# A scan without a barrier ahead of it: f32 spreads, paired sums, and the first scan tiles started inside the norm stage

## The chip, the cores and the metric

The kernel runs on one NeuronCore of one Trainium2 chip. The core has five engines with a queue each: PE (TensorE, matmuls into the eight PSUM banks), DVE (VectorE), ACT (ScalarE), POOL (GpSimd) and SP (which issues DMAs here). They run side by side and wait for each other through semaphores only. The metric is device time in microseconds from the first to the last instruction of one execution. Lower is better.

## The reference, cut to what matters

```python
def ssm(seq, A, W_B, b_B, W_C, b_C, W_Delta, b_Delta, bias_Delta):
    Bm = seq @ W_B.T + b_B
    Cm = seq @ W_C.T + b_C
    Delta = jax.nn.softplus(seq @ W_Delta.T + b_Delta + bias_Delta)
    A_bar = jnp.exp(A[None, None] * Delta[..., None])
    B_bar = 1.0 / A * (A_bar - 1.0) * Bm[..., None, :]
    # state = state * A_bar + x[..., None] * B_bar;  y = sum over the 16 states of state * Cm
...
x = sequence                                   # 1 x 4096 x 256, f32
x = x + ssm(layernorm(x), ...)                 # 256 channels of 16 states each, 4096 steps
x = x + ffn(layernorm(x), ...)                 # sqrt((x @ cos)^2 + (x @ sin)^2)
x = x + attention(layernorm(x), ...)           # 16 heads of 16
x = x + ffn(layernorm(x), ...)
```

The change lies in the first line alone, the layer norm with its projections and the scan. All else is computed by the same instructions before and after.

## The kernel before, in words

**The norm stage** (`norm_and_project`, a block of its own with a barrier at its end) goes over the 4096 rows in 8 chunks of 512. DVE takes mean and deviation and normalises. PE turns the chunk (`turn`, L393, eight 128x128 transposes) and multiplies it by the weights of B, C and Delta (L408, six f32 products of 512 columns, the trace shows each f32 product as two rows). ACT copies the turned chunk out of PSUM (L330), then adds the biases on the way out of the projections (`outputs`, L344, three a chunk). Three more steps a chunk make the turned chunk into three bf16 parts, `mem.xp`, whose sum is the f32 value: ACT rounds (`high` L334, `middle` L338), POOL subtracts (`what_hi_leaves` L212), DVE subtracts (`low` L247). The softplus of Delta is made by quarters of 1024 steps: `minus_abs` on DVE (L254), Exp and Ln on ACT (L350, L354), `softplus` on DVE (L259). DVE also makes the angles of the FFN weights (`angles`, `in_range`, L278 to L289).

**The scan** (`scan_to_projection`) has 128 tiles, n = 0 to 127. A tile is 8 channels x 16 states on the 128 partitions and 1024 steps on the free axis. Tile n is quarter n // 32, and its channels are the group j = n % 32. 16 tiles make a half, which is one block of 128 output channels. Its steps for tile n are:

- `spread_x` (PE, L717): a 0/1 matrix copies the 8 channels of x onto 128 partitions, in PSUM. Six bf16 products (three parts, two banks). It goes to one pair of banks, `xr`, for nearly all tiles, so that spread m + 1 waits until DVE has read spread m (`w_done`).
- `times_b` (DVE, L969): w = spread x times B.
- decay (ACT, L871): exp(A Delta) into PSUM, and for the tiles that POOL takes, exp(A Delta) - 1 in SBUF (L857, L860).
- u = w (decay - 1): by POOL (L1113), or by DVE (`own_u`, L980) where n % 8 is 0, 3 or 6, and for the last tile.
- scan (DVE, L999), then hc = state times C (POOL, L1122).
- gather (PE, L749): a 128x32 matrix of 1 / A sums the 16 states of each channel into `yb`, two f32 products of 512 columns, four rows. Four tiles in turn add into the same 32 partitions.
- After 16 tiles ACT copies y (L833), PE turns it (`turn_y`, L728), DVE adds it to x (`add_y`, L964).

The order on each queue is the order of the code. DVE does scan n, then `own_u` of n + 1 if it is DVE's, then `times_b` of n + 4. Near the start of a half two `times_b` stand around one `own_u` (after scan 5 of the half). PE does spread n + 5, then gather n. The named functions `scan_before`, `spread_after` and `by_pool` set these distances.

Of the kernel before, what the change touches and what calls it, by code (L numbers as in the profile page):

```python
# [131 lines left out]
def norm_and_project(nc, mem, io):  # L132

    with ExitStack() as ctx:
        def sb(name, shape, dt):
            return ctx.enter_context(nc.sbuf_tensor(name, shape, dt))

        w_bcd = place(mem, 136, [DH, 3, P])
        bias = sb("bias_bcd", [P, 4], F32)
        recip_a = sb("recip_a", [P, NJ], F32)  # L140
        mask = sb("channel_mask", [P, CPT], F32)
        xn = place(mem, 112, [2, TPC, D])
        xnt = place(mem, 120, [2, DH, CH])
        rest = place(mem, 128, [2, DH, CH])
        std = sb("np_std", [P, NT, 1], F32)
        noise = place(mem, 140, [DH, 2, D])
        turns = place(mem, 144, [DH, 2, D])
        ang = mem.w_ffn[:].rearrange("p h (a o) -> p h a o", a=2)
        tp = ctx.enter_context(nc.psum_tensor("np_tp", [P, DH, CH], F32))
        pb = ctx.enter_context(nc.psum_tensor("np_proj", [P, 2, 3, CH], F32))  # L150
        (loaded, consts, pool_step, gather_step, sums_done, stats_done, std_ready, rstd_ready, xn_ready, t_ready, xnt_ready,
         hi_ready, rest_ready, mid_ready, lo_ready, proj_ready, proj_read, neg_ready, exp_ready, ln_ready, bias_ready,
         soft_added, angles_loaded, angle_step, table_step) = make_sems(
            nc, ctx, "np", "loaded consts poolstep gatherstep sums stats std rstd xn t xnt hi rest mid lo proj projread neg "
            "exp ln bias softadded anglesloaded anglestep tablestep")
        x_loaded = make_sems(nc, ctx, "np", " ".join(f"x{i}" for i in range(NC)))

        def tiles(i):
            return slice(i * TPC, (i + 1) * TPC)

        def cols(i):
            return slice(i * CH, (i + 1) * CH)

        def quarter(q):
            return slice(q * SC, (q + 1) * SC)

        with nc.Block() as block:
            @block.sync
            def _(sp):
                xv = io.x.rearrange("a (t p) d -> (a p) t d", p=P)  # L170
                for i in range(NC):
                    sp.dma_start(mem.x[:, tiles(i), :], xv[:, tiles(i), :]).then_inc(x_loaded[i], 16)
                    if i == 0:
                        sp.dma_start(w_bcd, io.w_bcd.rearrange("(h p) j c -> p h j c", p=P)).then_inc(loaded, 16)
                        sp.dma_start(bias[:], io.bias_bcd).then_inc(loaded, 16)
                        sp.dma_start(mem.a_scale[:], io.a_tiles).then_inc(loaded, 16)
                for n, (w, e) in enumerate(((io.theta, io.theta_noise), (io.phi, io.phi_noise))):
                    sp.dma_start(ang[:, :, n, :], w.rearrange("(h p) o -> p h o", p=P)).then_inc(angles_loaded, 16)
                    sp.dma_start(noise[:, :, n, :], e.rearrange("(h p) o -> p h o", p=P)).then_inc(angles_loaded, 16)

            @block.gpsimd
            def _(pool):
                steps = Chain(pool, pool_step)

# [22 lines left out]
                def what_hi_leaves(i):  # L207

                    pool.wait_ge(hi_ready, i + 1)
                    if i >= 2:  # L210
                        pool.wait_ge(lo_ready, i - 1)
# [403 lines left out]
def scan_to_projection(nc, mem, io, ctx):  # L615
# [91 lines left out]
    def tensor(pe):  # L707
# [23 lines left out]
        for n in range(4):  # L731
            spread_x(n)
# [1103 lines left out]
```

## Time and profile before

| What | us |
|---|---|
| median of 3 runs | 3477.23 (3475.85 to 3478.11) |
| profiled execution, its time | 3478.46 |
| its span, first to last instruction | 3476.6 |
| norm stage, until the barrier | 0 to 77.2 |
| first four scans begin at | 83.5, 88.0, 97.9, 102.4 |
| last scan begins at | 593.2 |
| all that follows (FFN, attention, FFN) | about 609 to 3476.6 |

The table is read from left to right as stages that follow each other. The trace gives for each instruction its start, its engine, its duration, and what ended the idle time of its engine before it.

### The profile page before, as it was taken

What the parts mean: (1) busy time and instruction counts of PE and PEld (TensorE: products, weight loads), DVE (VectorE), ACT (ScalarE), POOL (GpSimd) and SP (SyncE); (2) the same over time, 40 slices, a digit from 0 to 9 for tenths busy, and PEclk for the clock granted to TensorE, in tenths of its full rate; (3) what the DMA queues carried; (4) which work ended last, traced back from release to release, by engine and by line L of the source; (5) the groups of instructions that cost most, each with busy time, mean ns of one, the idle gap of its engine ahead of it and who ended that gap; (6) DMA issues with size and microseconds to landing.
All of it is one profiled execution on the core that took longest, in us unless ns stands there. A gap on an engine that the chain in (4) does not pass through costs nothing.

```text
span 3476.6 us, 59741 instructions
## 1 busy us (share of the span) xinstructions
PE 3330.3 (96%) x22826; PEld 1192.6 (34%) x22852; DVE 3260.1 (94%) x4960; ACT 2718.5 (78%) x4991; POOL 830.4 (24%) x707
## 2 busy tenths in 40 slices
PE   6788888989999999999999999999999999999999
PEld 3222222542333333333333333333333333333334
DVE  7899999589999999999999999999999999999943
ACT  6766665756888888888888888888888888888865
POOL 3899998662000000000000000000000000000004
PEclk9999999988999999999999999999999999999999
DMA  2000001052020120202020202112020202020011
GB/s 65 1 10 0 1 1 49 31 149 30 6 33 13 28 30 10 33 6 33 8 33 6 33 6 33 25 16 33 6 33 6 36 6 33 6 33 6 8 55 49
DMA packets 53678, 87.11 MB, mean 25 GB/s; under 512 B 13200, under 2 KB 40464, under 8 KB 49232
## 3 DMA queue, kind: packets, MB, share of 16 engines
q1 hardware_dynamic: 53200, 82.77, 12.6%
q8 instruction: 179, 2.93, 0.4%
q14 instruction: 107, 0.88, 0.1%
q10 hardware_dynamic: 192, 0.52, 0.1%
HBM read 53.37 MB, written 21.23 MB: 21 GB/s over the span
## 4 chain that ended last, share of the span: by engine, by line
PE 81%; DVE 10%; issue 4%; POOL 1%; ACT 1%; DMA 0%; DVEq 0%; SPq 0%; POOLq 0%; ACTq 0%
PE banks L1493 29%; PE banks L1450 16%; PE banks L1445 15%; PE banks L1408 11%; DVE arena L999 5%; PE banks L553 3%; DVE arena L969 3%; PE banks L1406 2%; PE banks L805 1%; DVE arena L1666 1%; DVE arena L980 1%; PE banks L797 1%; PE banks L1515 1%; POOL arena L1122 0%; POOL arena L1113 0%
## 5 line engine op out<-in xcount | busy, mean ns | idle before, releaser
L1649 DVE TENSOR_REDUCE arena<-banks 128x1 f32<-128x512 f32 x4032 | 2503.7, 683 | 19.1 <-PE banks L1408 15.5
L1623 ACT ACTIVATE arena<-banks 128x512 f32<-128x512 f32 x4096 | 2114.9, 602 | 417.0 <-PE banks L1445 409.5
L1445 PE MATMUL banks<-arena 64*128 64x512 bf16 x4032 | 1245.8, 379 | 0.0
L1450 PE MATMUL banks<-arena 35*128 35x512 bf16 x4032 | 1207.2, 378 | 0.6 <-DMA arena<-max_rows 0.4
L1493 PE MATMUL banks<-arena 128*32 128x512 f32 x8192 | 1090.8, 605 | 0.0
L1406 PE MATMUL banks<-arena 64*128 64x512 bf16 x2048 | 789.2, 387 | 22.9 <-DVE arena L1666 20.2
L1408 PE MATMUL banks<-arena 64*128 64x512 bf16 x2048 | 786.9, 386 | 0.6 <-DVE arena L1649 0.6
L1445 PEld LDWEIGHTS banks<-arena 64*128 64x128 bf16 x4032 | 375.8, 93 | 391.7 <-PE banks L1450 5.7
L1408 PEld LDWEIGHTS banks<-arena 64*128 64x128 bf16 x2048 | 188.2, 93 | 796.6 <-DVE arena L1649 792.4
L1450 PEld LDWEIGHTS banks<-arena 35*128 35x128 bf16 x4032 | 358.0, 93 | 157.7 <-ACT arena L1623 8.7
L1373 POOL TENSOR_TENSOR arena<-arena 64x512 f32<-64x512 f32 x64 | 81.2, 1268 | 1191.6 <-DMA arena<-arena 1157.2
L1122 POOL TENSOR_TENSOR arena<-arena 128x1024 f32<-128x1024 f32 x128 | 301.7, 2369 | 30.3 <-DVE arena L999 30.0
L1341 POOL CAST neg_parts<-neg_max 128x8 bf16<-128x8 f32 x64 | 12.2, 191 | 1239.3 <-DVE neg_max L1661 1239.3
L999 DVE TENSOR_TENSOR_SCAN arena<-banks,carry,arena 128x1024 f32<-128x1024 f32 x128 | 299.2, 2338 | 1.0 <-POOL arena L1122 1.0
L749 PE MATMUL banks<-arena 128*32 128x512 f32 x512 | 247.7, 607 | 41.2 <-POOL arena L1122 41.2
L871 ACT ACTIVATE banks<-arena,a_scale 128x1024 f32<-128x1024 f32 x128 | 142.8, 1116 | 142.3 <-DVE arena L999 141.6
L1493 PEld LDWEIGHTS banks<-arena 128*32 128x32 f32 x8192 | 161.2, 108 | 237.9 <-issue 230.8
L717 PE MATMUL banks<-arena 128*128 128x512 bf16 x742 | 189.6, 389 | 51.7 <-DVE arena L969 39.2
L1406 PEld LDWEIGHTS banks<-arena 64*128 64x128 bf16 x2048 | 190.9, 94 | 52.8 <-DVE arena L1666 26.8
L1113 POOL TENSOR_TENSOR arena<-arena 128x1024 f32<-128x1024 f32 x79 | 189.0, 2393 | 15.3 <-DVE arena L969 15.3
L969 DVE TENSOR_TENSOR arena<-banks,arena 128x1024 f32<-128x1024 f32 x128 | 154.0, 1204 | 11.9 <-PE banks L717 11.9
L717 PEld LDWEIGHTS banks<-arena 128*128 128x128 bf16 x768 | 65.9, 99 | 219.0 <-DVE arena L969 121.6
(137 smaller groups left out, 1730.7 us busy)
## 6 DMA issues: line engine op xcount, KB each, us to landing
arena<-qk_parts SPq DMA_DIRECT2D x242, 128.0 KB, 7.1
qk_parts<-arena SPq DMA_DIRECT2D x32, 384.0 KB, 2.6
arena<-arena SPq DMA_DIRECT2D x63, 128.0 KB, 2.3
x_res<-in_x SPq DMA_DIRECT2D x8, 512.0 KB, 7.9
arena<-in_trig SPq DMA_DIRECT2D x2, 2048.0 KB, 9.0
arena<-qk_parts SPq DMA_DIRECT2D x64, 64.0 KB, 10.9
att_t<-arena SPq DMA_DIRECT2D x128, 32.0 KB
arena<-att_t SPq DMA_DIRECT2D x8, 512.0 KB, 5.5
```

What stands on the lines that cost most here:

```text
L717: last = nc.tensor.matmul(x_bank(n)[:, b * CH:(b + 1) * CH], mem.spread[:, j % NJH, :], mem.xp[:, part, j // NJH, c * SC + b * CH:c * SC + ...
L749: last = nc.tensor.matmul(yb[32 * g:32 * g + 32, b * CH:(b + 1) * CH], mem.gather[:, j, :], hc[:, n % 2, b * CH:(b + 1) * CH], start=(r == ...
L969: nc.vector.tensor_tensor(w[:, n % WBUF, :], x_bank(n), mem.b_rep[:, cols(n)], ALU.mult).then_inc(w_done, 1)
L999: nc.vector.tensor_tensor_scan(st[:, n % 2, :], decay[:, n % 2, :], w[:, n % WBUF, :], mem.carry[:, j:j + 1], ALU.mult, ALU.add).then_inc( ...
L1122: nc.gpsimd.tensor_tensor(hc[:, n % 2, :], st[:, n % 2, :], mem.c_rep[:, cols(n)], ALU.mult).then_inc(hc_done, 1)
L1406: return nc.tensor.matmul(out, q_twin[LANE:P, par, q], k_twin[LANE:P, par, c // 2, :], start=True, stop=True)
L1408: return nc.tensor.matmul(out, q_rows[0:LANE, par, q], k_rows[0:LANE, par, c * CH:(c + 1) * CH], start=True, stop=True)
L1445: return nc.tensor.matmul(sc[:, (4 * t + j) % SB, :], k, q, start=(j == 1), stop=(j != 1))
L1450: return nc.tensor.matmul(sc[:, (4 * t + j) % SB, :], k, q, start=(j != 1), stop=(j == 1))
L1493: last = nc.tensor.matmul(acc[32 * j:32 * j + VW, :], v_ones[:, h % 2, 2 * kp + j // 2, :], prob[:, t % PBUF, j * CH:(j + 1) * CH], start= ...
L1623: nc.scalar.activation(prob[:, t % PBUF, j * CH:(j + 1) * CH], sc[:, n % SB, :], ACT.Exp, scale=SCALE).then_inc(exp_done, 1)
L1649: nc.vector.tensor_reduce(part_max[:, b % 2, u // NC, u % NC:u % NC + 1], mx[:, unit_bank(b, u), :], AXX, ALU.max).then_inc(dve_read, 1)
```

## The change

It does these things:

1. The barrier between norm stage and scan is gone. The norm stage is now the first part of the one block that holds all else, and its semaphores (`mem.norm`) order the seam. It uses the PSUM banks of the scan: projections in banks 0 to 5, turned chunks in 6 and 7.
2. The turned chunk stays f32 in `mem.x_t`, and ACT copies it there straight from PSUM. `high`, `middle`, `what_hi_leaves` and `low` are gone. A spread is two f32 products (four rows) where it was six bf16 products.
3. At the seam PE does spread 0 (into banks 6 and 7) ahead of the projection of chunk 7. ACT does decay 0 ahead of the `outputs` of chunk 7. `minus_abs` of the last quarter moves behind scan 1 on DVE.
4. u of tile 1 is DVE's, so u of the first two tiles is.
5. The 16 tiles of a half run in another order of channel groups (`channels`): tile n and n + 1 now sum into different 32 partitions of `yb`. The gathers of two tiles stand together, bank by bank, behind the odd one (`sum_pair`), and hc has four buffers for two.

```diff
@@ norm_and_project
-            nc.scalar.activation(xnt[:, i % 2], tp[:], ACT.Copy).then_inc(xnt_ready, 1)
-        def high(i):
...
+        act.wait_ge(t_ready, i + 1)
+        nc.scalar.activation(mem.x_t[:, :, cols(i)], tp, ACT.Copy).then_inc(xnt_ready, 1)
...
             if i + 1 < NC:
                 turn(i + 1)
+            if i + 1 < NC:
+                project(pe, i)
@@ scan_to_projection
-    return n % 8 not in BY_DVE and n < NT_SCAN - 1
+    return n % 8 not in BY_DVE and 1 < n < NT_SCAN - 1
+def channels(n):
+    return n % NJ // NJH * NJH + n % 4 * 4 + n % NJH // 4
-        return yb if n in (1, 3) else xr
+        return yb if n in (0, 1, 3) else xr
@@ tensor
             for b in range(SC // CH):
-                for part in range(NPART):
-                    last = nc.tensor.matmul(
-                        x_bank(n)[:, b * CH:(b + 1) * CH], mem.spread[:, j % NJH, :],
-                        mem.xp[:, part, j // NJH, c * SC + b * CH:c * SC + (b + 1) * CH],
-                        start=(part == 0), stop=(part == NPART - 1))
+                last = nc.tensor.matmul(
+                    x_bank(n)[:, b * CH:(b + 1) * CH], mem.spread[:, j % NJH, :],
+                    mem.x_t[:, j // NJH, c * SC + b * CH:c * SC + (b + 1) * CH], start=True, stop=True)
...
-        for n in range(4):
-            spread_x(n)
+        pe.wait_ge(mem.norm.consts, 3)
+        spread_x(0)
+        mem.norm.project(pe, NC - 1)
+        spread_x(1)
+        pe.wait_ge(mem.norm.proj_read, NC)
+        spread_x(2)
+        spread_x(3)
...
+            if n % 2 == 1:
+                sum_pair(n - 1, n)
+        def sum_pair(*pair):
...
+            pe.wait_ge(hc_done, n + 1)
...
             for b in range(SC // CH):
-                last = nc.tensor.matmul(
-                    yb[32 * g:32 * g + 32, b * CH:(b + 1) * CH], mem.gather[:, j, :],
-                    hc[:, n % 2, b * CH:(b + 1) * CH], start=(r == 0), stop=(r == 3),
-                    tile_position=(0, 32 * g))
+                for m in pair:
+                    g, r = channels(m) % NJH // 4, channels(m) % 4
+                    last = nc.tensor.matmul(
+                        yb[32 * g:32 * g + 32, b * CH:(b + 1) * CH], mem.gather[:, channels(m), :],
+                        hc(m)[:, b * CH:(b + 1) * CH], start=(r == 0), stop=(r == 3), tile_position=(0, 32 * g))
@@ scalar
+            if n < 2:
+                act.wait_ge(mem.norm.proj_read, NC - 1 + n)
             soft_here(n)
...
+            if n == 0:
+                mem.norm.outputs(act, NC - 1)
@@ vector
         times_b(0)
         own_u(0)
-        times_b(1)
...
-            if own and len(ahead) == 2:
+            if own and len(ahead) >= 2:
                 times_b(ahead.pop(0))
...
+            if n == 1:
+                mem.norm.minus_abs(dve, NSC - 1)
@@ gpsimd
-            if n >= 2:
-                pool.wait_ge(y_done, n - 1)
+            if n >= 4:
+                pool.wait_ge(y_done, n - 3)
```

PE at the seam, before: L408 is the last two projections, L717 spreads, L749 gathers.

```order
14 L408 MATMUL np_proj<-arena 128x512 x12
15 L167 UNCONDITIONAL_BRANCH
16 L1775 UNCONDITIONAL_BRANCH
17 L717 MATMUL banks<-arena 128x512 x30
18 L749 MATMUL banks<-arena 32x512 x2
19 L717 MATMUL banks<-arena 128x512 x12
20 L749 MATMUL banks<-arena 32x512 x2
```

The same place after: L187 is a projection, L693 spreads, L735 gathers.

```order
14 L187 MATMUL banks<-arena 128x512 x6
15 L693 MATMUL banks<-arena 128x512 x2
16 L187 MATMUL banks<-arena 128x512 x6
17 L693 MATMUL banks<-arena 128x512 x12
18 L735 MATMUL banks<-arena 32x512 x4
19 L693 MATMUL banks<-arena 128x512 x4
20 L735 MATMUL banks<-arena 32x512 x4
```

Spread 0 now stands between the projections of chunks 6 and 7, there is no branch to another block, and seven spreads in all come before the first gathers, of which there are then two tiles' at once.

DVE at the seam, before: L247 is `low`, L254 `minus_abs`, L259 `softplus`, L969 `times_b`, L980 `own_u`, L999 the scan.

```order
54 L259 SCALAR_TENSOR_TENSOR arena<-arena 128x1024 x2
55 L247 TENSOR_TENSOR arena<-arena 128x2x512
56 L254 SCALAR_TENSOR_TENSOR arena<-arena 128x1024
57 L167 UNCONDITIONAL_BRANCH
58 L1785 UNCONDITIONAL_BRANCH
59 L969 TENSOR_TENSOR arena<-banks,arena 128x1024
60 L980 SCALAR_TENSOR_TENSOR arena<-banks,arena 128x1024
61 L969 TENSOR_TENSOR arena<-banks,arena 128x1024
62 L999 SCALAR_TENSOR_TENSOR arena<-banks,carry,arena 128x1024
63 L969 TENSOR_TENSOR arena<-banks,arena 128x1024 x2
```

The same place after: L172 is `minus_abs`, L964 `times_b`, L975 `own_u`, L995 the scan.

```order
47 L259 SCALAR_TENSOR_TENSOR arena<-arena 128x1024 x2
48 L964 TENSOR_TENSOR arena<-banks,arena 128x1024
49 L975 SCALAR_TENSOR_TENSOR arena<-banks,arena 128x1024
50 L995 SCALAR_TENSOR_TENSOR arena<-banks,carry,arena 128x1024
51 L964 TENSOR_TENSOR arena<-banks,arena 128x1024
52 L975 SCALAR_TENSOR_TENSOR arena<-banks,arena 128x1024
53 L964 TENSOR_TENSOR arena<-banks,arena 128x1024 x2
54 L995 SCALAR_TENSOR_TENSOR arena<-banks,carry,arena 128x1024
55 L964 TENSOR_TENSOR arena<-banks,arena 128x1024 x2
56 L172 SCALAR_TENSOR_TENSOR arena<-arena 128x1024
57 L995 SCALAR_TENSOR_TENSOR arena<-banks,carry,arena 128x1024
```

`low` and one `minus_abs` no longer stand ahead of the first `times_b`; three `times_b` and an `own_u` stand between scan 0 and scan 1.

PE in the steady state, around a `turn_y`, before (L728) and, in the second piece, after (L703):

```order
51 L717 MATMUL banks<-arena 128x512 x6
52 L749 MATMUL banks<-arena 32x512 x2
53 L728 MATMUL banks<-ident,arena 128x128 x8
54 L749 MATMUL banks<-arena 32x512 x2
55 L717 MATMUL banks<-arena 128x512 x12
56 L749 MATMUL banks<-arena 32x512 x2
57 L717 MATMUL banks<-arena 128x512 x6
```

```order
33 L693 MATMUL banks<-arena 128x512 x4
34 L735 MATMUL banks<-arena 32x512 x4
35 L703 MATMUL banks<-ident,arena 128x128 x8
36 L693 MATMUL banks<-arena 128x512 x4
37 L735 MATMUL banks<-arena 32x512 x4
38 L693 MATMUL banks<-arena 128x512 x4
39 L735 MATMUL banks<-arena 32x512 x4
```

Spreads of two tiles now follow one another with no gather between, except around the odd tiles, and nothing stands between `turn_y` and the spread that waits for `add_y`.

## Rows read from the trace of the kernel before

**Rows 1.** Stages: start:end, length, busy us (instructions) of each engine, granted clock (1.00 is full).

```profile
core 0: us, PE busy (x) PEld busy (x) DVE busy (x) ACT busy (x) POOL busy (x), PEclk, DMA share, GB/s
77.20:105.80 28.60, 21.09 (x58) 6.13 (x60) 20.59 (x15) 18.68 (x20) 17.11 (x8) 0.81 0.00 1
139.50:581.00 441.50, 377.54 (x1157) 103.10 (x1178) 438.47 (x277) 291.19 (x343) 423.09 (x182) 1.00 0.01 2
```

**Rows 2.** Costliest groups of the page: busy us, mean ns of one | idle before, releaser.

```profile
L999 DVE TENSOR_TENSOR_SCAN arena<-banks,carry,arena 128x1024 f32<-128x1024 f32 x128 | 299.2, 2338 | 1.0 <-POOL arena L1122 1.0
...
L871 ACT ACTIVATE banks<-arena,a_scale 128x1024 f32<-128x1024 f32 x128 | 142.8, 1116 | 142.3 <-DVE arena L999 141.6
...
L969 DVE TENSOR_TENSOR arena<-banks,arena 128x1024 f32<-128x1024 f32 x128 | 154.0, 1204 | 11.9 <-PE banks L717 11.9
```

**Rows 3.** Timeline of the seam: start, duration, engine, line, operation, [idle before <-releaser].

```profile
48.45 5.32 PE L408 MATMUL np_proj<-arena 128*128 128x512 f32 x12
...
54.93 1.07 PE L393 MATMUL np_tp<-ident,arena 128*128 128x128 f32 x8 [1.16 <-issue]
...
62.74 1.28 ACT L354 ACT_TABLE_LOAD   x1
62.87 5.39 PE L408 MATMUL np_proj<-arena 128*128 128x512 f32 x12 [1.72 <-ACT arena L344]
...
64.04 2.00 ACT L354 ACTIVATE arena<-arena 128x1024 f32<-128x1024 f32 x2
...
70.50 1.84 ACT L344 ACTIVATE arena<-np_proj,bias_bcd 128x512 f32<-128x512 f32 x3
...
75.69 1.22 DVE L254 SCALAR_TENSOR_TENSOR arena<-arena 128x1024 f32<-128x1024 f32 x1
...
77.61 5.72 PE L717 MATMUL banks<-arena 128*128 128x512 bf16 x17 [9.35 <-PEq L167]
```

**Rows 4.** Timeline of the first tiles of the scan.

```profile
83.51 2.34 DVE L999 TENSOR_TENSOR_SCAN arena<-banks,carry,arena 128x1024 f32<-128x1024 f32 x1
...
83.75 2.36 POOL L1113 TENSOR_TENSOR arena<-arena 128x1024 f32<-128x1024 f32 x1 [14.32 <-DVE arena L969]
...
88.16 2.70 PE L717 MATMUL banks<-arena 128*128 128x512 bf16 x6 [3.04 <-DVE arena L969]
...
96.77 1.23 DVE L969 TENSOR_TENSOR arena<-banks,arena 128x1024 f32<-128x1024 f32 x1 [4.65 <-PE banks L717]
...
102.42 2.34 DVE L999 TENSOR_TENSOR_SCAN arena<-banks,carry,arena 128x1024 f32<-128x1024 f32 x1
```

**Rows 5.** Timeline of the steady state, around scan 5 of a half.

```profile
302.70 1.47 PE L717 MATMUL banks<-arena 128*128 128x512 bf16 x6 [1.65 <-DVE arena L969]
...
304.10 1.91 PE L749 MATMUL banks<-arena 128*32 128x512 f32 x4
304.82 1.20 DVE L969 TENSOR_TENSOR arena<-banks,arena 128x1024 f32<-128x1024 f32 x1
...
307.58 1.23 DVE L969 TENSOR_TENSOR arena<-banks,arena 128x1024 f32<-128x1024 f32 x1 [0.43 <-PE banks L717]
...
322.82 1.91 PE L749 MATMUL banks<-arena 128*32 128x512 f32 x4 [1.24 <-POOL arena L1122]
```

**Rows 6.** Timeline of the attention stage: one step's four products of 32 columns.

```profile
1500.96 1.06 PE L1493 MATMUL banks<-arena 128*32 128x512 f32 x8
```

**Rows 7.** Timeline of PE alone, at and after long idle times.

```profile
136.34 1.03 PE L717 MATMUL banks<-arena 128*128 128x512 bf16 x2 [3.42 <-DVE arena L969]
...
221.02 0.75 PE L717 MATMUL banks<-arena 128*128 128x512 bf16 x2 [3.02 <-DVE arena L969]
...
584.01 1.90 PE L749 MATMUL banks<-arena 128*32 128x512 f32 x4 [2.71 <-POOL arena L1122]
...
593.28 3.53 PE L749 MATMUL banks<-arena 128*32 128x512 f32 x4 [2.37 <-POOL arena L1122]
```

**Rows 8.** Timeline around a `turn_y` of the steady state.

```profile
358.36 1.09 PE L728 MATMUL banks<-ident,arena 128*128 128x128 f32 x8
...
360.49 1.20 DVE L964 TENSOR_TENSOR x_res<-banks,x_res 128x1024 f32<-128x1024 f32 x1
```

More of the change, by code:

```diff
@@ L729, in turn_y @@
             last.then_inc(y_turned, 1)
[L731 to L732 removed]
+        pe.wait_ge(mem.norm.consts, 3)
[5 more added lines that the diff above has]
+        spread_x(3)
+        pe.wait_ge(mem.norm.gather_step, 5)
         def scan_tile(n):
[L734 to L737 removed]
+            k = n // NJH
+            if n % NJH == 2 and k > 0:
                 turn_y(k, n + 5)
@@ L845, in soft_here @@
         def soft_here(n):
+            if n // NJ < LATE and n % NJ < 4:
+                act.wait_ge(mem.norm.soft_added, n // NJ + 1)
             if n // NJ >= LATE and n % NJ < 4:
@@ L884, in scalar @@
             if n == 7:
+                act.wait_ge(mem.norm.angle_step, 10)
                 nc.scalar.activation(mem.w_ffn[:], mem.w_ffn[:], ACT.Sin)
@@ L992, in scan_tile @@
                 dve.wait_ge(u_dve, n - pool_before(n) + 1)
+            if n == 0:
+                dve.wait_ge(mem.norm.consts, 3)
             if n >= 2:
@@ L1002, in scan_tile @@
                 add_y(k, (k - 1) // DH * TPS, (k - 1) % DH)
-            ahead = [m for m in range(2, NT_SCAN) if scan_before(m) == n]
+            ahead = [m for m in range(1, NT_SCAN) if scan_before(m) == n]
             own = n + 1 < NT_SCAN and not by_pool(n + 1)
-            if own and len(ahead) == 2:
+            if own and len(ahead) >= 2:
                 times_b(ahead.pop(0))
@@ L1752, in hybrid_kernel @@
         mem.soft = place(mem, 96, [NSC, SC])
-        mem.spread = place(mem, 160, [NJH, P], BF16)
+        mem.spread = place(mem, 32, [NJH, P])
         mem.gather = place(mem, 164, [NJ, 32])
@@ L1771, in _ @@
             def _(sp):
-                for part in (middle, last):
+                for part in (first, middle, last):
                     part[0](sp)
@@ L1776, in _ @@
             def _(pe):
-                for part in (middle, last):
+                for part in (first, middle, last):
                     part[1](pe)
@@ L1781, in _ @@
             def _(act):
-                for part in (middle, last):
+                for part in (first, middle, last):
                     part[2](act)
@@ L1786, in _ @@
             def _(dve):
-                for part in (middle, last):
+                for part in (first, middle, last):
                     part[3](dve)
@@ L1791, in _ @@
             def _(pool):
-                for part in (middle, last):
+                for part in (first, middle, last):
                     part[4](pool)
```

484 lines of the change are left out of this document (229 added, 255 removed).

## The prediction

> **What bounds the kernel now.** I read the table by stages first. From 139.5 to 581 us, the steady state of the scan, DVE is busy 438.47 of 441.5 us [rows 1]: nothing that PE, ACT or POOL does there is worth anything by itself, unless it makes DVE wait. The first 28.6 us of the scan are different: DVE is busy 20.59 us, and PE's granted clock is 0.81. Then the groups of the page: per tile DVE owes a scan of 2.34 us and a `times_b` of 1.20 us, and its idle time in front of `times_b` is only 11.9 us in all [rows 2]. Then the timeline of the seam: the last projection ends at 68.3, ACT's last `outputs` at 72.3, DVE's last `minus_abs` at 76.9, and PE's first spread begins at 77.61, after 9.35 us of idle time [rows 3]. That is the barrier and what is queued ahead of it. Last, the first tiles: scan 0 at 83.51, scan 3 only at 102.42 [rows 4], because the clock had fallen to half (six bf16 products take 2.70 us at 88.16, against 1.47 us in the steady state [rows 4, 5]).
>
> **Part 1, the seam.** I place the new order by hand, on the rows' durations. In the norm stage PE is the late engine: a projection of 5.32 us, of which 0.17 are the tail of its last row, and a turn of 1.04 (1.07 at 54.93, with 1.16 us of waiting for DVE ahead of it) [rows 3]. The steps that go (two roundings on ACT, POOL's and DVE's subtractions) lie beside that and are worth only this wait of about 1.2 us, and the 1.72 us of waiting for ACT ahead of the last projection [rows 3]. So projection 5 ends at 53.6, turn 7 at 54.5, projection 6 at 59.7, spread 0 (four f32 rows, 1.9) at 61.5, projection 7 at 66.6.
>
> ACT: Ln with its table load (1.28 + 2.00 [rows 3]) ends at 60.7, `outputs` 6 (1.84) at 62.5, the load back to Exp at 63.8, decay 0 (1.12 [rows 2]) at 64.9. DVE waits for ACT's Ln, does two `softplus` until 62.1, `times_b` 0 until 63.3, own u 0 until 66.1, so scan 0 begins at 66.1. `outputs` 7 ends at 68.5, after projection 7. Decay 1 ends at 69.7. Spread 1 ends at 68.4, spreads 2 and 3 at 70.5 and 72.2. DVE: `times_b` 1 at 68.4, own u 1 until 70.9, `times_b` 2 and 3 until 73.4, scan 1 until 75.7. Spread 4 and 5 each wait for a `times_b`: `times_b` 4 at 75.7, 5 at 78.8 to 80.0, the moved `minus_abs` (1.22 [rows 3]) to 81.1, scan 2, own u 3, `times_b` 6, and **scan 3 begins at about 85.6 against 102.42: 16.8 us earlier.** POOL's u of tile 2 (2.36 us [rows 4], from about 72.2) ends at 74.5 and is hidden, its cover is the chain over spread 5. u of tile 1 adds 1.2 us to DVE and takes 2.36 us of POOL and two ACT steps off the road to scan 1; it is in the sum above. If PE's clock falls here too, two or three spreads cost about 1.5 us more each; if DVE or ACT come late at 60 us nothing is lost until 61.5. Bounds: 13 to 18 us.
>
> **Part 2, a spread of f32.** No row shows this form with these operands. The nearest ones are f32 products of 512 columns: twelve rows in 5.32 us, which is 0.43 apart [rows 3], and four of 32 columns in 1.91 [rows 5]. So a spread takes 1.90 for 1.47 us. It is on DVE's path wherever the time between the end of one `times_b` and the start of the next is short. In an ordinary tile a scan lies between: 307.58 + 1.23 to the next needs at least 2.2 us, the spread then has 0.25 us to spare, and the cost is nothing. After scan 5 of a half only an own u lies between, and DVE already waits 0.43 us for PE [rows 5], seven times. There the whole 0.43 is paid, and because the pair of gathers now stands just ahead of that spread (it would end about 0.3 us after `w_done`) 0.3 more: 0.72 x 7 = **5.0 us**.
>
> **Part 3, gathers in pairs.** Two tiles' gathers are eight rows. In the attention stage eight such rows, in four different column groups, take 1.06 us, where eight one after another would take 3.6 [rows 6]. Here two groups are at work, so I take 4 x 0.43 + 0.17 = 1.9 us for two tiles, what one tile takes now [rows 5]. PE's sum per tile goes from 1.29 + 1.72 to 1.72 + 0.86 us. That saves DVE nothing. But the pair falls on the odd tile with a longer spread ahead of it: 1.83 + 1.87 = 3.7 us against a DVE cycle of 3.4 where no own u is in it. At 322.82 the gather waits for POOL anyway [rows 5]; where an odd one does, the next spread is some 0.1 to 0.2 late for DVE, three times a half. I take 0.2 us a half, **1.6 us**, bounds 0 and 4. POOL's hc has four buffers, and waits for no one.
>
> **Part 4, PE's clock.** This is the part that speaks against the change. In before the clock fell to half after idle times of PE of 3.04 us [rows 4], of 3.42 and of 3.02 us, and at the end of the scan once after 2.37 us, while 2.71 us passed without a fall [rows 7]. In the steady state before, a gather stands in nearly every such gap, and what is left is as short as 1.65 and 1.24 us [rows 5]. Now PE has idle times of 2.1 to 2.3 us at three places of each half: from the end of `turn_y` (358.36 + 1.09) to the end of `add_y` (360.49 + 1.20) [rows 8], where a gather stood until now, and behind the spreads of two even tiles in whose cycle DVE has an own u. That is some 23 places. A spread at half clock lasts 1.5 to 1.9 us more (2.70 for 1.47 in bf16 [rows 4]), and has 0.25 to 0.5 to spare: about 1.3 us each time. The lower bound is no fall, 0 us, the upper one is all 23, 30 us. Since these idle times are just under the shortest that made it fall, I take one in four, six falls, **8 us**.
>
> **Part 5, the end of the scan.** The gather of tile 126, 3.53 us at half clock [rows 7], no longer stands ahead of the FFN's first turn. It is done with tile 127, at no extra cost. PE may go into the FFN's first product at half clock instead. I take 1 us of gain, bounds 0 and 2. All behind it is the same code.
>
> **Sum:** -16.8 - 1.0 + 5.0 + 1.6 + 8 = -3.2 us on the span of 3476.6. The time outside the span is 1.9 us and does not change. The profiled execution (3478.46) is 1.2 us above the median, which is noise of the run, so I take the difference from the median: 3477.2 - 3.2 = **3474.0 us**.
>
> **The rivals.**
>
> A, *the clock stays up* (two falls at most). For it: the gaps are shorter than nearly all that made it fall, and 2.71 us passed. Then -11.2 plus 0 to 2.6: 3466 to 3469.
>
> B, *the clock rules the scan*, which is the slower side: the idle times of 2.1 to 2.3 us, at 23 places, let the clock fall nearly each time, the spread that follows comes 1.3 us late for DVE, and DVE has no slack. Break-even is at (11.2 / 1.3) = 9 falls, and the time is over 0.2% above before from 14. All 23: +19 us, 3496. For it: 2.37 us was enough once. Against it: that gap was longer than these, and 2.71 us once was not enough.
>
> C, *the pair does not run side by side*. Then the odd tile has 1.83 + 3.6 us of PE work against 3.4 to 4.5 us of DVE's cycle, and DVE waits 0.7 to 2.5 us for each odd tile, about 10 us a half as I go through the eight pairs: 80 us in all, less the 6.6 already counted: about +60, 3537. Against it: eight rows in 1.06 us [rows 6]. Beside this stands the Trainium skill, TensorE: Matmul & The Clock Gate, Part 3 (packing small matmuls): LDWEIGHTS overlaps with matmuls in flight only where the row group differs. A pair here differs in its column group alone, so by that sentence it would run in series and the kernel would take this rival's time. Row 1500.96 disagrees with it for this very form of product.
>
> D, *the early start does not happen*: some wait of the seam, most likely Ln or the table loads on ACT, holds decay 0 until projection 7 is out. Everything else stays, the gain at scan 3 falls to about 12 us, since scan 1 waits for chunk 7 in any case. 3479.
>
> **How the numbers follow.** My forecast (3 to 9 falls, 3470 to 3478) 42%, A 33%, B 15%, C 5%, D 5%. Something like 0.2%, 7 us, is what a measurement of this kernel can tell from no change. Faster by more than that: all but a little of A, and the lower edge of mine, 37%. Slower by more: half of B and C, with some of my unknowns in part 3, 14%. Within it 49%. The range leaves out C and the far half of B above, and little of A below: 3463 to 3488.
>
> **What would show it.** In the profile after: scan 0 at 66, scan 3 at 85 to 86 us, no idle time of PE over 3 us between 50 and 80. A spread of four rows in 1.9 us. A pair of eight gather rows in 1.9 us; 3.6 would be C. Idle time of DVE in front of `times_b` behind PE: about 1.15 us seven times; and at falls of the clock 1 to 1.5 us each, with a granted clock in the steady state of about 0.97 for 1.00. The last scan at 581 to 586 for 593.2. A spread faster than 1.9 us, or DVE's cycle getting longer without a wait, would make the working wrong, and so would a scan 3 later than 90.

## The result, and the profile after

| | before | changed |
|---|---|---|
| median (lowest to highest), us | 3477.11 (3475.85 to 3478.11) | 3508.51 (3507.13 to 3513.56) |
| span of the profiled execution, us | 3476.6 | 3507.8 |
| mean granted clock | 0.988 | 0.977 |
| scan 3 begins at | 102.4 | 88.2 |
| scan 127 begins at | 593.2 | 624.9 |
| from there to the end | 2883.4 | 2882.9 |

The changed kernel is slower, 31.4 us: the ratio is 1.0093, with an interval of 1.0076 to 1.0111. The forecast was 3474.0, and its range ended at 3488. The start of the scan brought 14.2 us. Between scan 3 and scan 127 46 us were lost. Behind the scan there are 0.5 us, which tell nothing: in the traces of all twelve kernels this stretch lasts from 2881.8 to 2885.1 us.

The seam, in the timeline of the changed kernel (start, duration, engine, line, operation, [idle before <-releaser]); L365 is a turn, L187 a projection, L693 a spread, L862 a decay, L964 `times_b`, L1111 POOL's u, L172 `minus_abs`, L995 the scan:

```profile
54.72 1.04 PE L365 MATMUL banks<-ident,arena 128*128 128x128 f32 x8
...
60.74 1.88 PE L693 MATMUL banks<-arena 128*128 128x512 f32 x4
...
62.46 5.31 PE L187 MATMUL banks<-arena 128*128 128x512 f32 x12
...
64.91 1.12 ACT L862 ACTIVATE banks<-arena,a_scale 128x1024 f32<-128x1024 f32 x1
...
67.39 2.35 DVE L995 TENSOR_TENSOR_SCAN arena<-banks,carry,arena 128x1024 f32<-128x1024 f32 x1
...
80.12 1.22 DVE L964 TENSOR_TENSOR arena<-banks,arena 128x1024 f32<-128x1024 f32 x1 [2.08 <-PE banks L693]
...
80.38 2.34 POOL L1111 TENSOR_TENSOR arena<-arena 128x1024 f32<-128x1024 f32 x1
...
81.26 2.53 DVE L172 SCALAR_TENSOR_TENSOR arena<-arena 128x1024 f32<-128x1024 f32 x1
...
88.22 2.33 DVE L995 TENSOR_TENSOR_SCAN arena<-banks,carry,arena 128x1024 f32<-128x1024 f32 x1
88.36 2.17 PE L693 MATMUL banks<-arena 128*128 128x512 f32 x3 [3.13 <-DVE arena L964]
```

PE's wait of 9.35 us [rows 3] is gone, and spread 0 runs between two projections. Against [rows 4] scan 0 is 16.1 us earlier and scan 3 14.2 us. But the clock still falls here: the last row has the idle time of 3.13 us ahead of it, as [rows 4] has 3.04.

The same stretch of the steady state, 140 to 560 us, of before (first) and of the changed kernel (second). The columns are those of [rows 1]:

```profile
140.00:560.00 420.00, 358.69 (x1102) 98.32 (x1123) 416.97 (x263) 279.87 (x331) 402.36 (x173) 1.00 0.01 2
```

```profile
140.00:560.00 420.00, 317.34 (x828) 95.70 (x824) 382.76 (x239) 252.00 (x304) 367.80 (x158) 0.92 0.01 2
```

DVE was busy all but 3 us of 420, and now 37 us of 420 are idle. The granted clock went from 1.00 to 0.92. Two groups of the page say who is waited for; the first answers to L969 in [rows 2]:

```profile
L964 DVE TENSOR_TENSOR arena<-banks,arena 128x1024 f32<-128x1024 f32 x128 | 155.3, 1213 | 49.6 <-PE banks L693 49.5
...
L693 PE MATMUL banks<-arena 128*128 128x512 f32 x512 | 288.3, 691 | 130.3 <-DVE arena L964 113.5
```

DVE waits 49.5 us for the spreads, where it waited 11.9. `times_b` and the scan themselves last as long as before (1213 against 1204 ns, 2339 against 2338). So DVE is not slower, it is kept waiting. In the timeline of PE alone, one half of the changed kernel (L703 `turn_y`, L735 the gathers):

```profile
297.30 1.09 PE L703 MATMUL banks<-ident,arena 128*128 128x128 f32 x8 [0.68 <-DVE arena L964]
...
300.76 3.65 PE L693 MATMUL banks<-arena 128*128 128x512 f32 x4 [2.37 <-DVE x_res L957]
...
305.73 1.98 PE L693 MATMUL banks<-arena 128*128 128x512 f32 x4 [1.32 <-DVE arena L964]
307.64 1.91 PE L735 MATMUL banks<-arena 128*32 128x512 f32 x8
309.48 1.98 PE L693 MATMUL banks<-arena 128*128 128x512 f32 x4
...
320.66 3.22 PE L693 MATMUL banks<-arena 128*128 128x512 f32 x4 [2.14 <-DVE arena L964]
323.81 2.32 PE L735 MATMUL banks<-arena 128*32 128x512 f32 x8
```

At full clock a spread lasts 1.98 us and a pair of gathers 1.91. Behind an idle time of 2.37 us and one of 2.14 us a spread lasts 3.65 and 3.22 us. And DVE in the same stretch:

```profile
304.45 1.23 DVE L964 TENSOR_TENSOR arena<-banks,arena 128x1024 f32<-128x1024 f32 x1 [1.58 <-PE banks L693]
...
311.50 1.23 DVE L964 TENSOR_TENSOR arena<-banks,arena 128x1024 f32<-128x1024 f32 x1 [1.33 <-PE banks L693]
...
323.92 1.23 DVE L964 TENSOR_TENSOR arena<-banks,arena 128x1024 f32<-128x1024 f32 x1 [1.05 <-PE banks L693]
328.09 1.22 DVE L964 TENSOR_TENSOR arena<-banks,arena 128x1024 f32<-128x1024 f32 x1 [0.69 <-PE banks L693]
```

The waits at 304.45 and 323.92 stand right behind the two slow spreads, and that at 328.09 is what is still late from them. The wait of 1.33 us at 311.50 has only spreads at full clock around it. It is the place of [rows 5] where DVE waited 0.43 us. From 95 to 640 us the clock records of this trace hold 23 stretches at half clock, those of before hold 3. PE has twenty idle times of 2.13 to 2.37 us between scan 3 and the end of the scan. Behind 17 of them the clock fell, behind three it stayed up. One of these three:

```profile
493.10 1.98 PE L693 MATMUL banks<-arena 128*128 128x512 f32 x4 [2.14 <-DVE arena L964]
```

### The profile page after: what moved, and what is told of

Same layout as the page of the kernel before. It is cut to its first block, busy times and chain, and to the rows that moved or that the text cites. A ratio compares the mean times of both kernels' runs of the same rounds, so it can differ in the third digit from the quotient of the medians.

```text
span 3507.8 us, 59213 instructions
## 1 busy us (share of the span) xinstructions
PE 3315.4 (95%) x22596; PEld 1199.6 (34%) x22596; DVE 3246.8 (93%) x4953; ACT 2700.1 (77%) x4973; POOL 811.0 (23%) x698
## 4 chain that ended last, share of the span: by engine, by line
PE 86%; DVE 9%; issue 4%; ACT 1%; POOL 1%; DMA 0%; DVEq 0%; SPq 0%; POOLq 0%; ACTq 0%
PE banks L1493 29%; PE banks L1450 16%; PE banks L1445 15%; PE banks L1408 11%; DVE arena L995 4%; PE banks L693 3%; PE banks L522 3%; DVE arena L964 2%; PE banks L1406 2%; PE banks L791 1%; PE banks L187 1%; DVE arena L1666 1%; DVE arena L975 1%; PE banks L735 1%; PE banks L783 1%
## 5 line engine op out<-in xcount | busy, mean ns | idle before, releaser
L1493 PE MATMUL banks<-arena 128*32 128x512 f32 x8192 | 1090.8, 605 | 0.0
L693 PE MATMUL banks<-arena 128*128 128x512 f32 x512 | 288.3, 691 | 130.3 <-DVE arena L964 113.5
L995 DVE TENSOR_TENSOR_SCAN arena<-banks,carry,arena 128x1024 f32<-128x1024 f32 x128 | 299.3, 2339 | 0.0
L862 ACT ACTIVATE banks<-arena,a_scale 128x1024 f32<-128x1024 f32 x128 | 143.0, 1117 | 198.0 <-DVE arena L995 197.8
L964 DVE TENSOR_TENSOR arena<-banks,arena 128x1024 f32<-128x1024 f32 x128 | 155.3, 1213 | 49.6 <-PE banks L693 49.5
L1111 POOL TENSOR_TENSOR arena<-arena 128x1024 f32<-128x1024 f32 x78 | 185.9, 2383 | 65.3 <-DVE arena L964 65.3
L693 PEld LDWEIGHTS banks<-arena 128*128 128x128 f32 x512 | 94.4, 204 | 306.9 <-DVE arena L964 208.7
L735 PE MATMUL banks<-arena 128*32 128x512 f32 x512 | 131.8, 638 | 5.0 <-POOL arena L1122 4.9
```

What stands on the lines that cost most here:

```text
L693: last = nc.tensor.matmul(x_bank(n)[:, b * CH:(b + 1) * CH], mem.spread[:, j % NJH, :], mem.x_t[:, j // NJH, c * SC + b * CH:c * SC + (b + ...
L964: nc.vector.tensor_tensor(w[:, n % WBUF, :], x_bank(n), mem.b_rep[:, cols(n)], ALU.mult).then_inc(w_done, 1)
L995: nc.vector.tensor_tensor_scan(st[:, n % 2, :], decay[:, n % 2, :], w[:, n % WBUF, :], mem.carry[:, j:j + 1], ALU.mult, ALU.add).then_inc( ...
L1111: nc.gpsimd.tensor_tensor(w[:, n % WBUF, :], less[:, m % 2, :], w[:, n % WBUF, :], ALU.mult).then_inc(u_pool, 1)
L1493: last = nc.tensor.matmul(acc[32 * j:32 * j + VW, :], v_ones[:, h % 2, 2 * kp + j // 2, :], prob[:, t % PBUF, j * CH:(j + 1) * CH], start= ...
```

## The experiments

Two theories stood against each other. *The clock*: what is lost between scan 3 and scan 127 is lost because PE falls to half clock behind idle times that a gather used to fill. *The products*: it is lost because the f32 spreads, and the pairs ahead of them, are longer work on DVE's path at any clock.

| run | what it is | median, us | ratio to before (interval) | clock | falls |
|---|---|---|---|---|---|
| changed | | 3508.51 | 1.0093 (1.0076 to 1.0111) | 0.977 | 23 |
| e1_warm | changed, zero products in the gaps | 3476.96 | 1.0000 (0.9991 to 1.0010) | 0.988 | 5 |
| e2_barrier | changed, barrier back | 3509.89 | 1.0096 (1.0081 to 1.0111) | 0.976 | 23 |
| e3_single | changed, gathers one by one | 3479.76 | 1.0007 (0.9998 to 1.0016) | 0.990 | 2 |
| e4_pairs_before | before, with the pairs alone | 3493.89 | 1.0047 (1.0030 to 1.0064) | 0.976 | 14 |
| e5_f32_only | e2 and e3 together | 3484.88 | 1.0020 (1.0010 to 1.0029) | 0.991 | 2 |
| e6_warm_short | e1, half as many zero products | 3477.34 | 0.9998 (0.9989 to 1.0007) | 0.987 | 5 |
| e7_better | e1, later pair and halves | 3475.97 | 0.9995 (0.9986 to 1.0004) | 0.988 | 4 |
| e8_warm_barrier | e1, barrier back | 3480.42 | 1.0008 (0.9999 to 1.0017) | 0.986 | 5 |
| e9_warm_split | e6, halves alone | 3472.21 | 0.9984 (0.9975 to 0.9993) | 0.987 | 4 |
| e10_single_split | e3, halves | 3480.03 | 1.0004 (0.9995 to 1.0013) | 0.991 | 2 |

Each ratio is to before on the same chip, whose median there was 3477.03 (e1 to e4), 3477.85 (e5 to e8) and 3478.21 us (e9, e10). The clock is the mean of the profiled execution, and falls are stretches at half clock between 95 and 640 us (3 in before). A stretch is not a unit of time: one lasts 3.4 to 17.1 us. A difference between runs on two chips carries an error of about 1 us, since before itself has medians from 3477.03 to 3478.21.

### The gaps filled: e1_warm and e6_warm_short

```diff
 def scan_tile(n) of PE, behind turn_y and the spread
+            if n % NJH in (2, 6, 14) and 2 < n < 120:
+                add_zeros(n % NJH // 4 * 2 % 4)
...
+        def add_zeros(g):
+            for b in range(2):          # e6: range(1)
+                nc.tensor.matmul(yb[32 * g:32 * g + 32, b * CH:(b + 1) * CH], mem.zeros[:],
+                                 mem.x_t[:, 0, b * CH:(b + 1) * CH], start=False, stop=False,
+                                 tile_position=(0, 32 * g))
```

> The changed kernel, plus two f32 products of 512 columns with a zero weight matrix of 32 columns at the three places of each half where PE's idle time is over 2 us (before the spread of tile 7, and behind those of tiles 11 and 19 of the half). They add zero to a sum that is open, nothing waits for them. Theory 1 (the clock): the 41 us that DVE waits around falls of the granted clock go; the falls within the scan drop from 24 to about 3, and the time to 3473 (3468 to 3480). Theory 2 (the longer f32 spread and the pair are late for DVE whatever the clock): the waits stay, 3500 to 3515, since PE has more to do than before.

At three places of each half PE does products whose weights are zero, added into `yb`: work with no result, all else as in the changed kernel. In PE's timeline (L730 the zero products, L694 the spread, L704 `turn_y`, L745 the gathers):

```profile
286.91 1.09 PE L704 MATMUL banks<-ident,arena 128*128 128x128 f32 x8 [0.68 <-DVE arena L974]
287.93 1.90 PE L730 MATMUL banks<-arena,zeros 128*32 128x512 f32 x4
290.37 1.96 PE L694 MATMUL banks<-arena 128*128 128x512 f32 x4 [0.54 <-DVE x_res L967]
...
293.65 1.98 PE L694 MATMUL banks<-arena 128*128 128x512 f32 x4 [1.33 <-DVE arena L974]
295.56 1.91 PE L745 MATMUL banks<-arena 128*32 128x512 f32 x8
```

The spread behind `turn_y` starts when `add_y` lets it, as before, but takes 1.96 us where it took 3.65. On the page DVE's wait for the spreads falls from 49.5 to 19.2 us:

```profile
L974 DVE TENSOR_TENSOR arena<-banks,arena 128x1024 f32<-128x1024 f32 x128 | 155.0, 1211 | 19.3 <-PE banks L694 19.2
```

The median falls by 31.5 us, and from scan 3 to scan 127 e1 needs 504.7 us, against 536.7 in the changed kernel and 490.8 before. That splits the loss of 46 us: 32.0 us hang on the clock, and 13.9 remain with the clock up nearly throughout (e1 still has 5 falls, before has 3). PE has more to do in e1 than in the changed kernel, so the amount of work on PE is not what cost the 32 us.

> As e1_warm with one zero product (two rows, 0.86 us) at each of the three places for two. PE's idle time there is then about 1.2 us for 0.3. If it is the length of the idle time that counts, and 1.65 us was harmless in the kernel before, this holds the clock as well as e1: 3475 to 3479, 3 to 6 falls in the scan. If falls come by something else that the zeros only happened to fix (the tile position, the order), more falls and 3485 to 3500.

e6 has one product a place, two rows, for two products, and gives 3477.34 with 5 falls, the same as e1 within the intervals. The shorter of the two fillings is enough.

### The gathers one by one: e3_single

```diff
 def scan_tile(n) of PE
-            if n % 2 == 1:
-                sum_pair(n - 1, n)
+            sum_pair(n)
```

> The changed kernel with each tile's gathers alone behind its spread, as before the change, the new order of the channel groups kept. Theory 1 (the idle times of PE that the pairs leave make the clock fall): a gather stands in each gap again, the falls drop to 3 to 5 and their 41 us go; PE has 3.7 us a tile against 3.4 of DVE's shortest cycle, so some new waits, 5 to 15 us: 3472 to 3485. Theory 2 (PE has too much to do with f32 spreads): PE's sum per tile grows by 0.86 us, DVE's waits grow, 3510 to 3540.

This undoes the pairs and keeps f32, the channel order and the early start. No work is added against the changed kernel, each gather only stands again behind every spread. 3479.76 us, 28.7 below the changed kernel, and 2 falls. So it was the pairing that opened the gaps. What is left of the loss, 506.7 us from scan 3 to scan 127 for 490.8 before, is mostly waiting for the spreads. The DVE timeline of e3 shows it at the same place of a half (L963 `times_b`):

```profile
298.89 1.23 DVE L963 TENSOR_TENSOR arena<-banks,arena 128x1024 f32<-128x1024 f32 x1 [1.32 <-PE banks L693]
...
302.63 1.22 DVE L963 TENSOR_TENSOR arena<-banks,arena 128x1024 f32<-128x1024 f32 x1 [0.27 <-PE banks L693]
```

### The pairs alone, on before: e4_pairs_before

```diff
 before, def scan_tile(n) of PE, with the changed kernel's channels and sum_pair
+            if n % 2 == 1:
+                sum_pair(n - 1, n)
 gpsimd
-            if n >= 2:
-                pool.wait_ge(y_done, n - 1)
+            if n >= 3:
+                pool.wait_ge(y_done, n - 2)
```

> The kernel before, with only the pairs and the new order of the channel groups (three buffers for hc): bf16 spreads and the barrier stay. Theory 1: PE's gaps are even longer (2.6 us), the clock falls 20 times or more, but a bf16 spread at half clock is 1.2 us late with 0.65 us to spare, so about 0.6 us each: 3485 to 3497. Theory 2 (the f32 spread is what costs): DVE's slack is what it was, 3474 to 3479.

bf16 spreads, the barrier, and a third hc buffer. 3493.89 us, 16.9 slower than before, with 14 falls and no f32 spread at all. The pairs do it without the rest of the change. It costs about half of what it costs in the changed kernel. That doesn't come from less time at half clock: the 14 stretches are longer, 92 us in all, where the 23 of the changed kernel make 99. The bf16 spread that is slowed is shorter, which fits, but no run separates it. In PE's timeline (L726 spreads, L763 gathers) two places with the same idle time ahead of them come out differently:

```profile
153.06 2.74 PE L726 MATMUL banks<-arena 128*128 128x512 bf16 x6 [3.04 <-DVE arena L983]
155.73 3.51 PE L763 MATMUL banks<-arena 128*32 128x512 f32 x8
...
169.93 2.29 PE L726 MATMUL banks<-arena 128*128 128x512 bf16 x5 [2.37 <-DVE x_res L978]
...
256.06 1.47 PE L726 MATMUL banks<-arena 128*128 128x512 bf16 x6 [3.04 <-DVE arena L983]
```

An idle time of 3.04 us made it fall at 153 and not at 256. So the length of the one gap doesn't decide alone. Of the eleven idle times of 3.04 us that this trace has in the scan, the clock fell behind six.

### The barrier back: e2_barrier, e5_f32_only, e8_warm_barrier

```diff
 norm_and_project: chunk 7 and minus_abs again at the end of the stage
+        minus_abs(dve, NSC - 1)
+        outputs(act, NC - 1)
-            if i + 1 < NC:
-                project(pe, i)
+            project(pe, i)
 the program: the norm stage in a block of its own
+        with nc.Block() as block:
+            block.tensor(lambda pe: first[1](pe))
...
```

> The changed kernel with the barrier back: projection and outputs of chunk 7 and the last minus_abs in a block of their own ahead of the scan; f32 spreads, pairs and u of tile 1 on DVE stay. Both theories: slower than the changed kernel by what the seam is worth, 12 to 17 us, so 3520 to 3526, with scan 3 at about 103 us for 88.2. If the seam were worth nothing in the end (given back later through the clock), 3508.

> The changed kernel with both the barrier back and each tile's gathers alone: what is left of the change is the f32 spread (and with it the norm stage without the three parts), u of tile 1 on DVE and the channel order. From e2 and e3: with the clock up, the seam's 4.8 us at scan 3 should now stay to the end, so 3479.8 + 5 = 3484 to 3486. If the barrier is worth nothing (1.4 us between e2 and the changed kernel), 3480 to 3482.

> e1_warm with the barrier back: the seam's worth where the clock stays up. At scan 3 the barrier cost 4.8 us (93.0 for 88.2 us) in e2. If that is kept to the end where no falls blur it: 3477 + 5 = 3480 to 3483. If 1.4 us as between e2 and the changed kernel: 3478.

With the barrier back scan 3 begins at 93.0 us in e2, from its DVE timeline, 4.8 us later than in the changed kernel:

```profile
92.99 2.34 DVE L993 TENSOR_TENSOR_SCAN arena<-banks,carry,arena 128x1024 f32<-128x1024 f32 x1
```

The end is 1.4 us later (3509.89 against 3508.51), less than the spread of the runs. The 12 to 17 us that were expected of e2 were wrong: most of what the seam won is there with the barrier too. Where the clock holds, the barrier is worth 3.5 us (3480.42 for e8, 3476.96 for e1, on two chips) and 5.1 us (3484.88 for e5, 3479.76 for e3, also on two chips). Against before on its own chip each time it is 2.6 and 4.3 us, and e8 against e6, on one chip but with different fillings, gives 3.1. At scan 3 the traces differ more: 94.8 for 86.4 in e8 and e1, 93.2 for 86.5 in e5 and e3. The norm stage itself ends earlier or later by some 2 us from one profiled execution to the next, so one pair of traces can't price the barrier. By the medians it is worth 3 to 5 us. The rest of what the seam won comes from what e2 also has: no bf16 parts to make, u of tile 1 on DVE. These two weren't separated.

e5 is the f32 form alone, with barrier and single gathers: 3484.88, 1.0020 of before (1.0010 to 1.0029). Its scan 3 begins at 93.2, 9.2 us ahead of before, and its scan 127 at 599.5, 6.3 us behind. The f32 form, with u of tile 1 on DVE and the new channel order, wins at the seam and loses about 15 us on the way.

### The wait at scan 9 of a half taken away: e7_better, e9_warm_split, e10_single_split

```diff
 e9: tensor, in spread_x; vector, in times_b (e6 otherwise)
+                if b == 0 and in_halves(n):              # n > NJH and n % NJH == 9
+                    last.then_inc(half_ready, 1)
...
+            if in_halves(n):
...
+                dve.wait_ge(half_ready, n // NJH)
+                nc.vector.tensor_tensor(w[:, n % WBUF, 0:CH], x_bank(n)[:, 0:CH], mem.b_rep[:, lo], ALU.mult)
+                dve.wait_ge(xr_ready, n + 1)
+                nc.vector.tensor_tensor(w[:, n % WBUF, CH:SC], x_bank(n)[:, CH:SC], mem.b_rep[:, hi],
+                                        ALU.mult).then_inc(w_done, 1)
 e7: the same on e1, and
-            if n % 2 == 1:
+            if n > NJH and n % NJH == 4:
+                sum_pair(n - 2, n - 1)
+            elif n % 2 == 1 and not (n > NJH and n % NJH == 3):
                 sum_pair(n - 1, n)
```

With the clock up the largest wait that comes back in each half is the 1.33 us in front of `times_b` of tile 9 of a half. In these kernels DVE begins with the first bank of that spread while PE does the second. e7 also puts the pair of tiles 2 and 3 behind the spread instead of ahead of it.

> e1_warm, and at the one place of each half where DVE waits 1.33 us for a spread with the clock up: the gathers of tiles 2 and 3 of the half stand behind the spread of tile 9 for ahead of it, and times_b of tile 9 is done in two halves of 512 columns, each as soon as its bank is there. The wait should fall from 1.33 to 0.1 to 0.4 us, seven times, less 0.06 us for the second instruction: 6 to 8 us, 3469 to 3471. If the place is not on the path (POOL or ACT is right behind), less than 3 us: 3474 to 3477.

> The changed kernel, with the short zero products of e6 (two rows each) and times_b of tile 9 of a half in two halves, but the gathers of tiles 2 and 3 where the change has them. In e7 the wait of 1.33 us went to 0.26, but 0.81 came up at the next tile, because the moved gathers then stood ahead of that tile's spread. Here the wait should be 0.4 to 0.6 and nothing come up behind it: 0.7 to 0.9 us seven times, 5 to 6 us under e1 and e6: 3471 to 3473. If the wait comes up again elsewhere, 3475 to 3477.

> e3 (each tile's gathers alone, no zero products) with times_b of tile 9 in two halves. e3 waits 1.32 us there and 0.27 at the next tile with the clock up. The split should take 0.8 us of it seven times: 3474 to 3476 for e3's 3479.8. If PE, at 3.8 us a tile with single gathers, is itself the bound of that stretch, nothing: 3479 to 3480.

DVE's timeline in e7 (L983 and L985 the halves, L991 the next `times_b`):

```profile
296.63 0.69 DVE L983 TENSOR_TENSOR arena<-banks,arena 128x512 f32<-128x512 f32 x1
...
297.49 0.69 DVE L985 TENSOR_TENSOR arena<-banks,arena 128x512 f32<-128x512 f32 x1 [0.17 <-PE banks L698]
...
301.24 1.23 DVE L991 TENSOR_TENSOR arena<-banks,arena 128x1024 f32<-128x1024 f32 x1 [0.81 <-PE banks L698]
```

The wait at tile 9 falls from 1.33 to 0.26 us, but 0.81 us stand at the next tile, whose spread now has the moved pair ahead of it. 3475.97, no different from before. e9 leaves the pair in place:

```profile
296.15 0.69 DVE L981 TENSOR_TENSOR arena<-banks,arena 128x512 f32<-128x512 f32 x1 [0.47 <-PE banks L698]
...
297.01 0.69 DVE L983 TENSOR_TENSOR arena<-banks,arena 128x512 f32<-128x512 f32 x1 [0.17 <-PE banks L698]
297.62 2.34 DVE L1020 TENSOR_TENSOR_SCAN arena<-banks,carry,arena 128x1024 f32<-128x1024 f32 x1
299.88 1.20 DVE L989 TENSOR_TENSOR arena<-banks,arena 128x1024 f32<-128x1024 f32 x1
```

0.64 us of waiting where there were 1.33, and nothing behind it. A half takes 63.4 us from scan to scan (63.9 in e1). **3472.21 us against 3478.21 on its chip, 0.9984 (0.9975 to 0.9993)**: this version is faster than both kernels, by 6 us (0.16%) against before and by 36 to 37 us against the changed one, which was measured apart from it. In e10, with single gathers, the same halves save 0.6 us at tile 9 and 0.80 us appear at the next tile (0.27 in e3). 3480.03 against 3479.76 in e3: no gain. There the single gather stands ahead of the next spread. So the pairs are an advantage, once their gaps are filled: e9 is 7.8 us faster than e10 on the same chip.

## Why the prediction was wrong

It failed in one step of part 4, "I take one in four, six falls, 8 us", and in the price beside it. What happened is the mechanism of rival B, which had 15%.

**Part 4, the clock.** The places were right: the step named the gap behind `turn_y` and those behind two even spreads, 2.1 to 2.3 us each, some 23 in all. The trace has them at 2.37 and 2.14 us. The number of falls was wrong: 17 of the twenty such idle times made the clock fall, where one in four was taken. With six others, behind idle times of 1.96 to 4.55 us and at the end of the scan, that makes 23 stretches; that this equals the step's count of places is chance. The rows before held only one idle time in this range, 2.37 us, and it made the clock fall; one of 2.71 us did not [rows 7]. The trace of before has another, which no row shows, and behind which the clock stayed up:

```profile
122.70 1.24 PE L717 MATMUL banks<-arena 128*128 128x512 bf16 x5 [2.22 <-DVE arena L969]
```

From two rows that contradict each other I took "just under the shortest that made it fall" as if the length of a gap decided alone. e4 shows that it doesn't (3.04 us with both outcomes), and in the changed kernel an idle time of 2.99 us at 124.94 passed while most of 2.14 us did not. No row of before gives a rate like 17 in twenty. The price was wrong as well: e1 has 5 falls and needs 32.0 us less, 29.9 of it idle time of DVE, which is about 1.8 us for each of the 18 others, for 1.3 expected. The step counted the slow spread alone. The pair of gathers behind it is slow too (2.32 for 1.91 us at 323.81), so a second `times_b` is late (0.69 us at 328.09, where e1 waits 0.20). The term is 32 us, where 8 were taken, and it is above the 30 us that the step gave for its own upper end.

**Part 1, the seam.** Right in its mechanism, 2.6 us short: 14.2 for 16.8. Scan 0 came at 67.4 for 66.1. PE was 1.3 us late already at turn 7, which ends at 55.8 for 54.5, and stayed so: projection 7 ends at 67.8 for 66.6. This half of the miss belongs to the one profiled execution: e1, e3, e6, e7, e9 and e10 have the same norm stage, and their scan 0 comes at 64.8 to 65.8. The other half is in the working. From scan 0 to scan 3 the changed kernel, e1, e6, e7 and e9 all take 20.8 us, for 19.5 forecast. There `minus_abs` took 2.53 us for the 1.22 that its row before showed, beside POOL's u of tile 3 at 80.38, which ends at 82.7. Its row before has POOL idle [rows 3, 4]. In e1, e6, e7 and e9 it takes 2.53 or 2.54 us at the same place. In e3 it falls just behind that u, and takes 1.22 us:

```profile
78.12 2.34 POOL L1110 TENSOR_TENSOR arena<-arena 128x1024 f32<-128x1024 f32 x1
...
80.91 1.22 DVE L172 SCALAR_TENSOR_TENSOR arena<-arena 128x1024 f32<-128x1024 f32 x1
```

The working moved the step, and took its duration along from a place where POOL did nothing. 14.2 lies inside the bounds of 13 to 18. "No idle time of PE over 3 us between 50 and 80" held, but the gap of 3.13 us came right after, at 88.

**Parts 2 and 3, the longer spread and the pair.** The two durations were right: 1.98 for 1.90 us, and 1.91 for 1.9. The wait at the tight place is 1.33 us for the 1.15 forecast. But together they cost 13.9 us from scan 3 to scan 127 (e1 against before) for 6.6. Of these, 11.9 are idle time of DVE (from scan 3 to scan 127 all its gaps over 0.05 us add up to 19.6 us in e1, 7.7 before). The tight place has 0.9 us more, seven times: 6.3. In a half of e1 two more waits of 0.2 us stand in front of a `times_b`, about 2.8 in all. The other 2.8 lie in the first 28 tiles, where e1 has three stretches at half clock (the first of them ahead of 95 us). The rest, 2 us, is no waiting: `times_b` is 8 ns longer each, 1 us in all, and 1 us stays open. So the sum was too small in three places: the tight place (6.3 for 5.0), the tiles behind a pair (2.8 for 1.6), and the first tiles and the longer `times_b`, for which it had no term. "In an ordinary tile the spread has 0.25 us to spare, and the cost is nothing" holds where no gather stands ahead of the spread. In e1 the waits of 0.2 us are behind a pair, which ends half a microsecond after DVE is done with the `times_b` before (246.77 + 1.20):

```profile
246.56 1.91 PE L745 MATMUL banks<-arena 128*32 128x512 f32 x8
246.77 1.20 DVE L974 TENSOR_TENSOR arena<-banks,arena 128x1024 f32<-128x1024 f32 x1
...
248.40 1.98 PE L694 MATMUL banks<-arena 128*128 128x512 f32 x4
...
250.42 1.22 DVE L974 TENSOR_TENSOR arena<-banks,arena 128x1024 f32<-128x1024 f32 x1 [0.20 <-PE banks L694]
```

In e3 a single gather stands there and costs the same 0.2. All in all e3, without pairs, waits nearly as long for the spreads: 21.7 us, against 11.9 before.

```profile
L963 DVE TENSOR_TENSOR arena<-banks,arena 128x1024 f32<-128x1024 f32 x128 | 155.2, 1212 | 21.7 <-PE banks L693 21.7
```

**Part 5, the end.** From scan 127 on the time is 2882.9 us for 2883.4: 0.5 us gained for 1, inside its bounds. The twelve traces differ here by 3.3 us, so neither value is confirmed.

**The sum with the measured terms** is -14.2 + 13.9 + 32.0 - 0.5 = +31.2 us. It must give the difference of the two spans, since it is made from them; what is measured by a run is the split of 45.9 into 13.9 and 32.0.

**The rivals.** A, the clock stays up, would have given 3466 to 3469. e1 is that case made by hand, and gives 3476.96: A was too low, mostly by parts 2 and 3. B was right in its mechanism, with 3496 still too low. C is refuted: eight gather rows in two column groups take 1.91 us. The sentence of the Trainium skill that stood beside it (TensorE: Matmul & The Clock Gate, Part 3), that weight loads overlap with matmuls in flight only where the row group differs, is not what this trace shows for f32 products of 32 columns. The prediction took it to mean that a pair runs in series; the same part's table of measured speedups has three column tiles at 2.38 times, and that is the way the pair came out here. At half clock, too, the pair at 155.73 in e4 takes 3.51 us, what a single gather took at 593.28 before [rows 7]. D did not come about: decay 0 ran at 64.91, 2.9 us ahead of the end of projection 7.

## What to carry to other kernels

An edit that saves PE time in a stage where PE mostly waits wins little there (e1 is 2.8 us faster than e3, which has single gathers), and it can lose more: 28.7 us between the changed kernel and e3. It turns filled gaps into empty ones, and the work behind them can run at half clock. Before such an edit, list the gaps it opens and price all of them at half clock as the likely case, with the work behind the first late instruction counted too. Where the gaps can't be avoided, a few products with zero weights can hold the clock. On an engine with idle time they were as good as free: e1 with four rows at each place and e6 with two gave the same time.

## What the runs showed of the hardware

- In the changed kernel the clock fell to half behind 17 of twenty idle times of PE of 2.13 to 2.37 us, and stayed up behind three of the same length and behind one of 2.99 us. 3.04 us did both in one kernel (e4). Something besides the length of the idle time decides, and no run measured what.
- Two rows of zero products at the three gaps of over 2 us in each half (e6) were enough to bring the falls from 23 to 5. In e9 a spread with 1.39 us of idle time behind the zero product ran at full clock:

```profile
285.52 1.05 PE L736 MATMUL banks<-arena,zeros 128*32 128x512 f32 x2
...
287.96 1.96 PE L698 MATMUL banks<-arena 128*128 128x512 f32 x4 [1.39 <-DVE x_res L973]
```

- Eight f32 rows of 32 columns, in two column groups in turn, took 1.91 us, as four rows in one group did.
- `minus_abs`, a `scalar_tensor_tensor` of DVE with all operands in SBUF, took 2.53 us where POOL was in the middle of a product, and 1.22 us where that product had just ended. It ended 1.1 us behind POOL's product, as if it had begun when that was over. Ten traces bear it out: 2.53 or 2.54 us in the changed kernel, e1, e6, e7 and e9, where POOL is at work, and 1.22 or 1.23 us in e2, e3, e5, e8 and e10, where it is not. `times_b` and own u, which read PSUM, stay at 1.19 to 1.23 us beside POOL.
